# The causal mask of the row maxima: from TensorE's accumulation to VectorE's maximum pass, with another order of steps

## The chip, the cores and the metric

The kernel runs on one core of a Trainium2 chip. The time is device time in microseconds (us) from one launch to its end; the lower the better. Every time below was measured on the chip, and every row comes from one profiled execution.

## What is computed

Cross attention with a causal mask and a residual, then a feed-forward layer with a residual, for x and a context of shape (16, 512, 512) in fp32, 16 heads of width 32. Cut to what matters here:

```python
scores = einsum('bhsd,bhtd->bhst', qh, kh) * scale
mask = triu(ones((Sq, Sq), dtype=bool), k=0).at[0, 0].set(False)   # the diagonal is masked too, but for (0, 0)
scores = where(mask, -inf, scores)
probs = softmax(scores, axis=-1)
out = einsum('bhst,bhtd->bhsd', probs, vh)
x = x + (out @ Wo.T + bo)          # q from layernorm(x), k and v from the context
x = x + ffn(layernorm(x))          # ternary weights, relu squared; not touched by the change
```

## The kernel before

The kernel has two phases, one after the other: attention for all 16 batches (`attention_phase`), then the feed-forward layer for all 16 (`ffn_phase`). Only the first is touched.

**Two passes over the scores.** The 16 heads are worked in 4 groups of 4. For each group the scores are computed twice. The first pass (steps `S`, function `s_unit`) has queries on the partitions and is used only for the maximum of every row. The maxima of a group, 16 columns of `maxima`, are then transposed by TensorE (step `M`, L637), split into a high and a low part by ScalarE (L707) and VectorE (L768), and sent by two DMAs (step `SEND`, L711) into rows 96 and 97 of the stacked operands. The second pass (steps `T`, `t_unit`, L534) has keys on the partitions, subtracts the maximum by those two rows, and goes through ScalarE's exponential (L742) and a mask on GpSimd (L435) into `probs`; steps `PV` multiply by V.

**A score unit.** Only blocks on or below the diagonal are computed. They are packed into units of 512 columns, one PSUM bank each, 10 units a group (`UNITS`), 40 a batch. In a half group (two heads) units 0 and 2 hold the 512 columns of a head's last query block, units 1 and 3 hold 384 and 128 columns (its third and its first block), and unit 4 holds 256 columns of each head (the second block). The same pattern of columns repeats for units 5 to 9. The two banks `s_bank` alternate: TensorE may start unit u once VectorE has signalled `s_free` for unit u-2.

**Where the mask is.** After the score products of a unit, TensorE accumulates `ident_bf` times `masks` (bf16, entries 0 or -1e30) onto the blocks at the diagonal (L513): 128 columns in units 0 and 2, 256 in the others. VectorE then takes maxima from PSUM with `tensor_reduce`: one of 512 (L804), or 384 and 128 (L807, L808), or one over two runs of 256 (L811).

**The order.** Each engine runs the same list of steps, `batch_steps` (written out by hand, L59 to L88), and picks out its own work; each engine is in order, and semaphores tie them together. VectorE's list passes through `low_parts_later`, which moves the low part (L778) of a Q, K, XT or CT step behind the next `S` step where such a step comes soon. `PART` is a third of a Q, K or V product (4 of its 12 matmuls), so that score units can stand between the thirds. `STACK` (SyncE) copies Q and K from `stage` into the stacked operands with six DMAs for two heads (L353); `S` units 0 and 5 of a group wait for them. `ONES`, `NT`, `NR`, `NB`, `NM`, `NH`, `NL` are the normalisation by the row sums (`NT` L831, `NR` L834, `NB` L838), `LN_*` and `XT`/`CT` prepare the next batch, `OA`/`OC`/`OB` are the output projection. So ("S", 3, 4) is unit 4 of group 3.

Of the kernel before, what the change touches and what calls it, by code (L numbers as in the profile page):

```python
# [12 lines left out]
P = 128  # L13
# [4 lines left out]
MASKED = -1e30  # L18
UNITS = 10
# [36 lines left out]
def batch_steps(more):  # L56

    steps = [
# [3 lines left out]
        ("STACK", 1, 0), ("M", 0), ("V", 2), ("SEND", 0), ("PART", "Q", 2, 0), ("STACK", 1, 1), ("PART", "Q", 2, 1),  # L62
# [26 lines left out]
    ]  # L89
    return steps if more else [s for s in steps if not is_next(s, True) and s[0] not in ("X_LOAD", "C_LOAD")]  # L90
# [103 lines left out]
def attention_phase(nc, dram, batches):  # L194
# [14 lines left out]
    with ExitStack() as c:  # L209
# [25 lines left out]
        ident_bf = sb("ident_bf", [P, P], BF16)  # L235
        masks = sb("masks", [P, 3, P], BF16)
# [51 lines left out]
        CONSTS = 12  # L288
# [119 lines left out]
        def _(pool):  # L408
# [3 lines left out]
            consts.inc(pool.memset(ident_bf[:, :], 0.0))  # L412
            consts.inc(pool.memset(masks[:, :, :], 0.0))
# [3 lines left out]
            for m in (ident, ident_bf):  # L417
                consts.inc(pool.affine_select(out=m[:, :], in_=m[:, :], compare_op=ALU.not_equal, fill=1.0,
                                              base=0, pattern=[[-1, P]], channel_multiplier=1))

            consts.inc(pool.affine_select(out=masks[:, 2, :], in_=masks[:, 2, :], compare_op=ALU.is_ge, fill=MASKED,
                                          base=0, pattern=[[-(P + 1), P]], channel_multiplier=P))
            for m in range(2):
                consts.inc(pool.affine_select(out=masks[:, m, :], in_=masks[:, m, :], compare_op=ALU.is_ge,
                                              fill=MASKED, base=-1, pattern=[[-1, P]], channel_multiplier=1))
# [67 lines left out]
        def _(pe):  # L493
# [9 lines left out]
            def s_unit(g, k, out):  # L503
                st = stack[g % 2]
                pair, u = divmod(k, 5)

                def block(h, r, t1, cols, start=True):

                    pe.matmul(out[:, cols:cols + t1], st[0:96, QS, h, P * r:P * r + P], st[0:96, KS, h, 0:t1],  # L509
                              start=start, stop=False, skip_group_check=True)  # L510

                def mask(view, added):
                    return pe.matmul(view, ident_bf[:, :], added, start=False, stop=True, skip_group_check=True)  # L513

                if u < 4 and u % 2 == 0:
                    block(2 * pair + u // 2, 3, 512, 0)
                    return mask(out[:, 384:512], masks[:, 0, :])
                if u < 4:  # L520
                    block(2 * pair + u // 2, 2, 384, 0)
                    block(2 * pair + u // 2, 0, 128, 384, start=False)
                    return mask(out[:, 256:512], masks[:, 1:3, :].rearrange("p m x -> p (m x)"))
                block(2 * pair, 1, 256, 0)
                block(2 * pair + 1, 1, 256, 256, start=False)
                return mask(out[:, :].rearrange("p (h t) -> p h t", h=2)[:, :, P:2 * P], masks[:, 0:2, :])
# [889 lines left out]
```

## Time and profile before

| | |
|---|---|
| median of 3 runs | 2728.15 us (2727.88 to 2735.14) |
| the profiled execution, its own time | 2733.87 us |
| its span, first to last instruction | 2732.2 us |
| mean granted TensorE clock | 0.978 of full |
| TensorE matmuls, busy | 2611.6 us (96%) |
| VectorE busy | 1596.1 us (58%) |
| ScalarE busy | 1031.2 us (38%) |
| GpSimd busy | 840.9 us (31%) |

The attention phase fills roughly the first 1570 us of the span. Busy time of a matmul counts from its start to its modelled end, and neighbouring matmuls overlap; so what a matmul adds to the time is read from the distance between the ends of neighbours in a timeline, not from its duration. The same holds, to a smaller degree, for VectorE. In a timeline the first number is the start and the second the time taken; a row with "xN" merges N instructions.

### The profile page before, as it was taken

The numbers are of one execution on the slowest core, as the hardware profiler recorded it, in microseconds if no ns is written. First come the engines' busy times: TensorE is split into PE (matmuls) and PEld (weight loads), VectorE is DVE, ScalarE is ACT, GpSimd is POOL, SyncE is SP. The second block draws the span as 40 slices with busy tenths as digits, with TensorE's granted clock in tenths as the row PEclk, the third lists the DMA queues.
The fourth block names the chain that finished last, engine by engine and source line by source line (L and its number), as shares of the span: only waits on it lengthen the run. The fifth ranks groups of instructions, "written<-read, shape, count | busy, mean of one in ns | idle before, by whom it ended". The sixth has DMA issues, their size and how long they took to land. (4 is left out here: it accounts for less than half of the span.)

```text
span 2732.2 us, 45231 instructions
## 1 busy us (share of the span) xinstructions
PE 2611.6 (96%) x14258; PEld 1943.7 (71%) x14258; DVE 1596.1 (58%) x3166; ACT 1031.2 (38%) x1903; POOL 840.9 (31%) x1559
## 2 busy tenths in 40 slices
PE   7999999999999999999999949999999999999998
PEld 5676667667766766776676537888888888888887
DVE  4675676667667666766765474444444444444454
ACT  2433433343343334334433454333333333333332
POOL 1643654474356346445644600000000000000000
PEclk9999999999999999999999868999999999999999
DMA  4344254344435433533444240000000000000000
GB/s 149 84 123 124 68 148 116 91 102 130 117 75 141 116 104 89 141 113 82 128 116 112 52 156 16 31 31 31 31 31 31 31 31 31 31 31 31 31 31 31
DMA packets 125252, 215.58 MB, mean 79 GB/s; under 512 B 20244, under 2 KB 22292, under 8 KB 124709
## 3 DMA queue, kind: packets, MB, share of 16 engines
q1 hardware_dynamic: 121124, 214.14, 28.0%
q10 hardware_dynamic: 4096, 1.06, 0.2%
q8 instruction: 16, 0.26, 0.0%
q14 instruction: 16, 0.12, 0.0%
HBM read 79.86 MB, written 33.55 MB: 42 GB/s over the span
## 5 line engine op out<-in xcount | busy, mean ns | idle before, releaser
L742 ACT ACTIVATE probs<-bank 128x512 f32<-128x512 f32 x640 | 359.2, 596 | 316.0 <-PE bank L534 310.7
L1159 PE MATMUL y_bank<-projT,a_hi 128*128 128x512 f32 x1024 | 409.1, 399 | 0.0
L1147 PE MATMUL h_bank<-x2T_hi,fcT 128*128 128x512 f32 x1024 | 406.4, 397 | 0.9 <-ACT scale_row L1230 0.9
L1148 PE MATMUL h_bank<-x2T_lo,fcT 128*128 128x512 f32 x1024 | 406.9, 397 | 0.0
L1161 PE MATMUL y_bank<-projT,a_lo 128*128 128x512 f32 x1024 | 403.9, 394 | 0.0
L1074 POOL COPY x_res<-x_in_sb 128x512 f32<-128x512 f32 x64 | 53.7, 879 | 1030.4 <-DVE y_sb L1376 967.9
L1238 ACT ACTIVATE relu<-h_bank,scale_fc 128x512 f32<-128x512 f32 x256 | 175.9, 687 | 503.5 <-PE h_bank L1151 503.5
L1349 DVE CAST a_hi<-act_sq 128x512 fp32r<-128x512 f32 x256 | 120.8, 472 | 372.5 <-ACT act_sq L1243 372.5
L435 POOL TENSOR_SCALAR_AFFINE_SELECT probs<-probs 128x256 f32<-128x256 f32 (+1 forms) x640 | 228.1, 367 | 250.8 <-ACT probs L742 244.4
L509 PE MATMUL bank<-stack 96*128 96x512 f32 (+3 forms) x1024 | 268.9, 340 | 19.5 <-DMA stack<-stage 15.5
L534 PE MATMUL bank<-stack 98*128 98x512 f32 (+3 forms) x1024 | 267.4, 346 | 17.0 <-DMA stack<-m_stage 15.9
L804 DVE TENSOR_REDUCE maxima<-bank 128x1 f32<-128x512 f32 x256 | 175.9, 687 | 142.6 <-PE bank L513 139.2
L534 PEld LDWEIGHTS bank<-stack 98*128 98x128 f32 x1024 | 175.6, 196 | 91.5 <-ACT probs L742 47.0
L477 POOL TENSOR_TENSOR x_res<-x_res,bias_sb 128x512 f32<-128x512 f32 x64 | 80.4, 1288 | 519.1 <-DMA x_res<-in_x_dram 455.1
L509 PEld LDWEIGHTS bank<-stack 96*128 96x128 f32 x1024 | 180.1, 195 | 74.4 <-issue 31.2
L1148 PEld LDWEIGHTS h_bank<-x2T_lo,fcT 128*128 128x128 f32 x1024 | 193.3, 189 | 47.2
L1147 PEld LDWEIGHTS h_bank<-x2T_hi,fcT 128*128 128x128 f32 x1024 | 193.1, 189 | 47.3 <-issue 1.1
L1161 PEld LDWEIGHTS y_bank<-projT,a_lo 128*128 128x128 f32 x1024 | 192.4, 188 | 43.3
L1159 PEld LDWEIGHTS y_bank<-projT,a_hi 128*128 128x128 f32 x1024 | 192.4, 188 | 43.2
L727 ACT ACTIVATE stage<-bank 128x512 fp32r<-128x512 f32 x128 | 76.5, 598 | 314.5 <-PE bank L500 289.8
L453 POOL TENSOR_TENSOR acc<-probs 128x384 f32<-128x384 f32 x192 | 189.8, 1009 | 11.7 <-POOL probs L435 7.4
L1351 DVE TENSOR_TENSOR a_lo<-act_sq,a_hi 128x512 fp32r<-128x512 f32 x256 | 185.9, 726 | 8.8
(187 smaller groups left out, 4922.1 us busy)
## 6 DMA issues: line engine op xcount, KB each, us to landing
stack<-stage SPq DMA_DIRECT2D x768, 128.0 KB, 2.3
xc_rows<-in_x_dram SPq DMA_DIRECT2D x16, 1024.0 KB, 5.3
x_res<-in_x_dram SPq DMA_DIRECT2D x16, 1024.0 KB, 5.5
x<-x_res SPq DMA_DIRECT2D x64, 256.0 KB, 2.2
x_in_sb<-x SPq DMA_DIRECT2D x16, 1024.0 KB, 5.6
out_dram<-y_sb SPq DMA_DIRECT2D x64, 256.0 KB, 2.0
xc_rows<-in_ctx_dram SPq DMA_DIRECT2D x15, 1024.0 KB, 5.3
stack<-m_stage ACTq DMA_DIRECT2D x128, 8.0 KB, 2.2
```

What stands on the lines that cost most here:

```text
L435: return pool.affine_select(out=view, in_=view, compare_op=ALU.is_ge, fill=0.0, base=0 if first_block else -1, pattern=([[0, count]] if co ...
L453: chain.inc(pool.tensor_tensor(acc[:, h, P:S], probs[:, u0, P:S], probs[:, u1, 0:S - P], ALU.add))
L509: pe.matmul(out[:, cols:cols + t1], st[0:96, QS, h, P * r:P * r + P], st[0:96, KS, h, 0:t1], start=start, stop=False, skip_group_check=True)
L534: return pe.matmul(out[:, cols:cols + S - P * r], st[0:98, KS, h, P * r:P * r + P], st[0:98, QS, h, P * r:S], start=True, stop=True)
L742: act.activation(probs[:, s[2], :], t_bank[u % 2][:, :], ACT.Exp, scale=SCALE).then_inc(exp_done, 1)
L804: last = dve.tensor_reduce(maxima[:, col + 3:col + 4], bank_u[:, :], AX.X, ALU.max)
L1147: pe.matmul(h_bank[b % 2][:, :], fcT[:, k, cols], xT_hi[:, k, :], start=k == 0, stop=False)
L1148: pe.matmul(h_bank[b % 2][:, :], fcT[:, k, cols], xT_lo[:, k, :], start=False, stop=False)
L1159: pe.matmul(y_bank[j][:, :], a_hi[:, b % RING, P * j:P * j + P], projT[:, b, :], start=b == 0, stop=False)
L1161: last = pe.matmul(y_bank[j][:, :], a_lo[:, b % RING, P * j:P * j + P], projT[:, b, :], start=False, stop=b == NB - 1)
L1238: act.activation(relu[:, b % 2, :], h_bank[b % 2][:, :], ACT.Relu, scale=scale_fc[:, b:b + 1]).then_inc(relu_done, 1)
L1351: dve.tensor_tensor(a_lo[:, b % RING, :], act_sq[:, b % 2, :], a_hi[:, b % RING, :].bitcast(F32), ALU.subtract).then_inc(hid_ready, 1)
```

## The change

The 640 mask matmuls (40 a batch) are gone. `s_unit` now issues only score products, and each is a finished product of its own. VectorE adds the mask itself: each `tensor_reduce` becomes a `tensor_tensor_reduce` that adds a bf16 mask tile from SBUF (`causal`, of which the last 128 columns hold the triangle and the rest zeros, or `causal_first` for the first block), writes the sum back to the same PSUM columns, and leaves its maximum over the row in `maxima`. Unit 4 and unit 9, which one instruction covered before, take two. Each of these instructions is followed on VectorE by a second one that puts the accumulated maximum into its column. VectorE waits for `s_full` with a wait of its own ahead of the instruction (`wait_alone`).

The list of steps is written anew as well. Only pieces of it are shown.

```diff
-        ("STACK", 1, 0), ("M", 0), ("V", 2), ("SEND", 0), ("PART", "Q", 2, 0), ("STACK", 1, 1), ("PART", "Q", 2, 1),
-        ("T", 0, 0), ("T", 0, 1), ("X_LOAD",), ("S", 1, 0), ("S", 1, 1), ("Q", 2), ("T", 0, 2), ("S", 1, 2),
...
+        ("STACK", 1, 0), ("M", 0), ("V", 2), ("SEND", 0), ("PART", "Q", 2, 0), ("STACK", 1, 1), ("T", 0, 0),
+        ("PART", "Q", 2, 1), ("T", 0, 1), ("S", 1, 0), ("T", 0, 2), ("S", 1, 1), ("Q", 2), ("S", 1, 2), ("S", 1, 3),
...
-        ident_bf = sb("ident_bf", [P, P], BF16)
-        masks = sb("masks", [P, 3, P], BF16)
+        causal = sb("causal", [P, S], BF16)
+        causal_first = sb("causal_first", [P, P], BF16)
...
-                    block(2 * pair + u // 2, 3, 512, 0)
-                    return mask(out[:, 384:512], masks[:, 0, :])
+                    return block(2 * pair + u // 2, 3, 0)
...
-                    block(2 * pair + u // 2, 2, 384, 0)
-                    block(2 * pair + u // 2, 0, 128, 384, start=False)
-                    return mask(out[:, 256:512], masks[:, 1:3, :].rearrange("p m x -> p (m x)"))
-                block(2 * pair, 1, 256, 0)
-                block(2 * pair + 1, 1, 256, 256, start=False)
-                return mask(out[:, :].rearrange("p (h t) -> p h t", h=2)[:, :, P:2 * P], masks[:, 0:2, :])
+                    block(2 * pair + u // 2, 2, 0)
+                    return block(2 * pair + u // 2, 0, 384)
+                block(2 * pair, 1, 0)
+                return block(2 * pair + 1, 1, 256)
...
-                        dve.wait_ge(s_full, i * SB + u + 1)
+                        wait_alone(dve, dve_passed, (s_full, i * SB + u + 1))
+
+                        def row_max(h, r, cols):
+
+                            t1 = P * r + P
+                            added = causal_first[:, :] if r == 0 else causal[:, S - t1:S]
+                            return dve.tensor_tensor_reduce(
+                                out=bank_u[:, cols:cols + t1], in0=bank_u[:, cols:cols + t1], in1=added, scale=1.0,
+                                scalar=LOWEST, op0=ALU.add, op1=ALU.max,
+                                accum_out=maxima[:, 4 * h + r:4 * h + r + 1])
+
                         if k < 4 and k % 2 == 0:
-                            col = 4 * (2 * pair + k // 2)
-                            last = dve.tensor_reduce(maxima[:, col + 3:col + 4], bank_u[:, :], AX.X, ALU.max)
+                            last = row_max(2 * pair + k // 2, 3, 0)
                         elif k < 4:
-                            col = 4 * (2 * pair + k // 2)
-                            dve.tensor_reduce(maxima[:, col + 2:col + 3], bank_u[:, 0:384], AX.X, ALU.max)
-                            last = dve.tensor_reduce(maxima[:, col:col + 1], bank_u[:, 384:512], AX.X, ALU.max)
+                            row_max(2 * pair + k // 2, 2, 0)
+                            last = row_max(2 * pair + k // 2, 0, 384)
                         else:
-                            col = 8 * pair + 1
-                            last = dve.tensor_reduce(maxima[:, col:col + 5:4],
-                                                     bank_u[:, :].rearrange("p (h t) -> p h t", h=2), AX.X, ALU.max)
+                            row_max(2 * pair, 1, 0)
+                            last = row_max(2 * pair + 1, 1, 256)
                         last.then_inc(s_free, 1)
```

**Place A: TensorE, group 3, from unit 4 on.** L509 is a score product (banks 2 and 3 are the two score banks), L513 the mask, L534 (L526 after) a product of the second pass of group 2, L499 after and L500 before a product of Q for the next batch. Before:

```order
L509 MATMUL bank2<-stack1 128x256 x2
L513 MATMUL bank2<-masks,ident_bf 128x2x128
L534 MATMUL bank5<-stack0 128x512
L632 REGISTER_ALU
L509 MATMUL bank3<-stack1 128x512
L513 MATMUL bank3<-masks,ident_bf 128x128
L534 MATMUL bank4<-stack0 128x384
L534 MATMUL bank4<-stack0 128x128
L632 REGISTER_ALU
L509 MATMUL bank2<-stack1 128x384
L509 MATMUL bank2<-stack1 128x128
L513 MATMUL bank2<-masks,ident_bf 128x256
```

After, the same units 4, 5 and 6:

```order
L499 MATMUL bank1<-xT_hi,wT_hi 128x512
L499 MATMUL bank1<-xT_lo,wT_hi 128x512
L624 REGISTER_ALU
L509 MATMUL bank2<-stack1 128x256 x2
L526 MATMUL bank4<-stack0 128x384
L526 MATMUL bank4<-stack0 128x128
L624 REGISTER_ALU
L509 MATMUL bank3<-stack1 128x512
L624 REGISTER_ALU
L509 MATMUL bank2<-stack1 128x384
L509 MATMUL bank2<-stack1 128x128
L526 MATMUL bank5<-stack0 128x512
```

The second third of Q stood between units 7 and 8 before; now it stands ahead of unit 4, and from unit 4 to unit 9 at most one unit of the second pass stands between two score units.

**Place B: VectorE, group 2, up to the low part of the maxima (`m_stage`).** `stage` is the low part of K for group 3, `xT_lo` of x for the next batch, `o_recip` and `o_small` are `NT` and `NR` of group 0. Before:

```order
L807 TENSOR_REDUCE maxima<-bank2 128x1
L808 TENSOR_REDUCE maxima<-bank2 128x1
L801 REGISTER_ALU
L811 TENSOR_REDUCE maxima<-bank3 128x2
L777 REGISTER_ALU
L778 TENSOR_TENSOR stage<-bank0,stage 128x512
L777 REGISTER_ALU
L778 TENSOR_TENSOR xT_lo<-bank1,xT_hi 128x512
L767 REGISTER_ALU
L768 TENSOR_TENSOR m_stage<-bank2,m_stage 16x128
```

After, where the low part of K has just gone ahead of these rows:

```order
L799 ISA bank3,maxima<-bank3,causal 128x256
L799 ISA maxima 128x1
L799 ISA bank3,maxima<-bank3,causal 128x256
L799 ISA maxima 128x1
L769 REGISTER_ALU
L770 TENSOR_TENSOR xT_lo<-bank1,xT_hi 128x512
L827 ISA
L830 STREAM_TRANSPOSE o_recip<-bank7 128x512
L833 RECIPROCAL o_small<-o_recip 128x16
L759 REGISTER_ALU
L760 TENSOR_TENSOR m_stage<-bank2,m_stage 16x128
```

The low part of K moved from behind unit 9 to ahead of it, and `NT` and `NR` of group 0 moved from behind the low part of the maxima to ahead of it. Each of the two new instructions of unit 9 has a second one behind it.

## Rows read from the trace of the kernel before

**Rows 1.** Busy time by stretch: one batch, and group 3's units 0 to 9.

```profile
core 0: us, PE busy (x) PEld busy (x) DVE busy (x) ACT busy (x) POOL busy (x), PEclk, DMA share, GB/s
683.22:692.73 9.51, 9.23 (x57) 6.44 (x56) 7.86 (x16) 5.59 (x10) 6.89 (x14) 1.00 0.58 169
646.00:740.80 94.80, 91.94 (x582) 64.33 (x581) 63.30 (x127) 36.83 (x72) 48.20 (x92) 1.00 0.42 111
```

**Rows 2.** Groups by line, whole span: busy, mean ns | idle before.

```profile
L804 DVE TENSOR_REDUCE maxima<-bank 128x1 f32<-128x512 f32 x256 | 175.9, 687 | 142.6 <-PE bank L513 139.2
L513 PE MATMUL bank<-masks,ident_bf 128*128 128x256 bf16 (+1 forms) x640 | 170.6, 267 | 0.0
```

**Rows 3.** Timeline of TensorE, group 2: score units with their masks.

```profile
671.78 0.40 PE L534 MATMUL bank<-stack 98*128 98x384 f32 x2
672.02 0.45 PE L509 MATMUL bank<-stack 96*128 96x512 f32 x1
672.31 0.23 PE L513 MATMUL bank<-masks,ident_bf 128*128 128x128 bf16 x1
672.35 0.47 PE L500 MATMUL bank<-cT_lo,wT_hi 128*128 128x512 f32 x1
672.66 0.39 PE L500 MATMUL bank<-cT_hi,wT_lo 128*128 128x512 f32 x1
...
673.36 0.40 PE L509 MATMUL bank<-stack 96*128 96x384 f32 x2
673.60 0.28 PE L513 MATMUL bank<-masks,ident_bf 128*128 128x256 bf16 x1
673.64 0.48 PE L500 MATMUL bank<-cT_hi,wT_lo 128*128 128x512 f32 x1
```

**Rows 4.** Timeline of VectorE, group 0: four instructions with no idle between.

```profile
639.36 0.68 DVE L778 TENSOR_TENSOR stage<-bank,stage 128x512 fp32r<-128x512 f32 x1
639.96 0.55 DVE L807 TENSOR_REDUCE maxima<-bank 128x1 f32<-128x384 f32 x1
640.43 0.28 DVE L808 TENSOR_REDUCE maxima<-bank 128x1 f32<-128x128 f32 x1
640.62 0.69 DVE L811 TENSOR_REDUCE maxima<-bank 128x2 f32<-128x512 f32 x1
```

**Rows 5.** Timelines: small instructions of VectorE, an accumulator read of ScalarE.

```profile
9.04 0.38 DVE L166 BATCH_NORM_AGGREGATE ln_mean_var<-ln_stats 128x2 f32<-128x6 f32 x4
...
1594.73 0.61 ACT L1183 ACTIVATE relu<-w_nat 128x512 f32<-128x512 f32 x1
1595.25 0.18 ACT L1183 ACTIVATION_READ_ACCUMULATOR relu<-w_nat 128x1 f32 x1
```

**Rows 6.** Group of a VectorE instruction with two tensor sources and a scalar.

```profile
L1291 DVE SCALAR_TENSOR_TENSOR tern<-w_nat,half,neg 128x512 bf16<-128x512 f32 x12 | 8.5, 748 | 0.7 <-PE h_bank L1093 0.5
```

**Rows 7.** Timeline of TensorE: maxima transposed, then the second pass (groups 0, 3).

```profile
642.12 0.27 PE L637 MATMUL bank<-ident,maxima 128*128 128x128 f32 x1
...
646.81 0.64 PE L534 MATMUL bank<-stack 98*128 98x512 f32 x3
...
693.82 0.33 PE L637 MATMUL bank<-ident,maxima 128*128 128x128 f32 x1 [0.15 <-DVE maxima L811]
...
697.92 0.73 PE L534 MATMUL bank<-stack 98*128 98x512 f32 x3 [0.58 <-DMA stack<-m_stage]
```

**Rows 8.** Timelines of TensorE, VectorE and SyncE's queue: group 2 to 3.

```profile
674.42 0.39 PE L500 MATMUL bank<-cT_hi,wT_lo 128*128 128x512 f32 x1
676.74 1.06 PE L554 MATMUL bank<-probs,v_sb 128*32 128x512 f32 x8 [0.46 <-POOL probs L435]
680.86 0.50 PE L534 MATMUL bank<-stack 98*128 98x512 f32 x1 [0.31 <-DMA stack<-m_stage]
682.66 0.49 PE L509 MATMUL bank<-stack 96*128 96x512 f32 x1 [0.86 <-DMA stack<-stage]
...
675.81 0.68 DVE L778 TENSOR_TENSOR stage<-bank,stage 128x512 fp32r<-128x512 f32 x1
677.17 0.27 DVE L768 TENSOR_TENSOR m_stage<-bank,m_stage 16x128 fp32r<-16x128 f32 x1
...
676.76 7.25 SPq L353 DMA_DIRECT2D stack<-stage  x11
```

More of the change, by code:

```diff
@@ L18 @@
 MASKED = -1e30
+LOWEST = -3.0e38
 UNITS = 10
@@ L58, in batch_steps @@
     steps = [
[1 row of a table removed]
[1 row of a table added]
         ("Q", 1), ("S", 0, 3), ("S", 0, 4), ("PART", "K", 1, 0), ("S", 0, 5), ("PART", "K", 1, 1), ("S", 0, 6),
         ("K", 1), ("S", 0, 7), ("S", 0, 8), ("PART", "V", 1, 0), ("S", 0, 9), ("PART", "V", 1, 1), ("V", 1),
-        ("STACK", 1, 0), ("M", 0), ("V", 2), ("SEND", 0), ("PART", "Q", 2, 0), ("STACK", 1, 1), ("PART", "Q", 2, 1),
[26 rows of a table removed]
[4 rows of a table added]
+        ("T", 0, 8), ("PART", "V", 3, 0), ("STACK", 2, 0), ("T", 0, 9), ("LN_STATS", 1), ("LN_STATS", 2),
[22 rows of a table added]
     ]
@@ L286, in attention_phase @@
         act_passed = sem("act_passed")
-        CONSTS = 12
+        CONSTS = 10
         HI_SKIP = sum(s[0] == "V" for s in STEADY)
@@ L411, in _ @@
             consts.inc(pool.memset(ident[:, :], 0.0))
-            consts.inc(pool.memset(ident_bf[:, :], 0.0))
-            consts.inc(pool.memset(masks[:, :, :], 0.0))
+            consts.inc(pool.memset(causal[:, :], 0.0))
+            consts.inc(pool.memset(causal_first[:, :], 0.0))
             consts.inc(pool.memset(ones[:, :], 1.0))
@@ L416, in _ @@
             pool.wait_ge(consts_ready, consts.now())
[L417 to L425, printed above, removed]
+            consts.inc(pool.affine_select(out=ident[:, :], in_=ident[:, :], compare_op=ALU.not_equal, fill=1.0,
+                                          base=0, pattern=[[-1, P]], channel_multiplier=1))
+            consts.inc(pool.affine_select(out=causal_first[:, :], in_=causal_first[:, :], compare_op=ALU.is_ge,
+                                          fill=MASKED, base=0, pattern=[[-(P + 1), P]], channel_multiplier=P))
+            consts.inc(pool.affine_select(out=causal[:, S - P:S], in_=causal[:, S - P:S], compare_op=ALU.is_ge,
+                                          fill=MASKED, base=-1, pattern=[[-1, P]], channel_multiplier=1))
             for s in range(2):
@@ L505, in s_unit, with block @@
                 pair, u = divmod(k, 5)
[L507 to L513, printed above, removed]
+                def block(h, r, cols):
+                    t1 = P * r + P
+                    return pe.matmul(out[:, cols:cols + t1], st[0:96, QS, h, P * r:P * r + P], st[0:96, KS, h, 0:t1],
+                                     start=True, stop=True)
                 if u < 4 and u % 2 == 0:
-                    block(2 * pair + u // 2, 3, 512, 0)
-                    return mask(out[:, 384:512], masks[:, 0, :])
+                    return block(2 * pair + u // 2, 3, 0)
                 if u < 4:
-                    block(2 * pair + u // 2, 2, 384, 0)
-                    block(2 * pair + u // 2, 0, 128, 384, start=False)
-                    return mask(out[:, 256:512], masks[:, 1:3, :].rearrange("p m x -> p (m x)"))
-                block(2 * pair, 1, 256, 0)
-                block(2 * pair + 1, 1, 256, 256, start=False)
-                return mask(out[:, :].rearrange("p (h t) -> p h t", h=2)[:, :, P:2 * P], masks[:, 0:2, :])
+                    block(2 * pair + u // 2, 2, 0)
+                    return block(2 * pair + u // 2, 0, 384)
+                block(2 * pair, 1, 0)
+                return block(2 * pair + 1, 1, 256)
             def t_unit(g, k, out):
@@ L800, in program @@
                         pair, k = divmod(s[2], 5)
-                        dve.wait_ge(s_full, i * SB + u + 1)
+                        wait_alone(dve, dve_passed, (s_full, i * SB + u + 1))
+                        def row_max(h, r, cols):
+                            t1 = P * r + P
+                            added = causal_first[:, :] if r == 0 else causal[:, S - t1:S]
[3 more added lines that the diff above has]
+                                accum_out=maxima[:, 4 * h + r:4 * h + r + 1])
                         if k < 4 and k % 2 == 0:
-                            col = 4 * (2 * pair + k // 2)
-                            last = dve.tensor_reduce(maxima[:, col + 3:col + 4], bank_u[:, :], AX.X, ALU.max)
+                            last = row_max(2 * pair + k // 2, 3, 0)
                         elif k < 4:
-                            col = 4 * (2 * pair + k // 2)
-                            dve.tensor_reduce(maxima[:, col + 2:col + 3], bank_u[:, 0:384], AX.X, ALU.max)
-                            last = dve.tensor_reduce(maxima[:, col:col + 1], bank_u[:, 384:512], AX.X, ALU.max)
-                        else:
-                            col = 8 * pair + 1
-                            last = dve.tensor_reduce(maxima[:, col:col + 5:4],
-                                                     bank_u[:, :].rearrange("p (h t) -> p h t", h=2), AX.X, ALU.max)
+                            row_max(2 * pair + k // 2, 2, 0)
+                            last = row_max(2 * pair + k // 2, 0, 384)
+                        else:
+                            row_max(2 * pair, 1, 0)
+                            last = row_max(2 * pair + 1, 1, 256)
                         last.then_inc(s_free, 1)
```

51 rows, old and new, of the table steps are left out of this document.

## Prediction

> **What bounds the kernel now.** I read the page first (which engine is busy, and where), then the busy time by stretch, then the groups by line, and last the timelines around the score units. The stretch of one batch [rows 1] is 94.8 us long; TensorE is busy in 91.94 of it at the full clock (granted 1.00, its 2.4 GHz level), VectorE in 63.3, ScalarE in 36.8. So in the attention phase TensorE is the bound, idle for 2.9 us a batch, and VectorE has a third of its time free. That free time is not even: while group 3's ten score units run, VectorE is busy 7.86 us out of 9.51 [rows 1], 83%. What comes off TensorE comes off the time, unless VectorE is late where the units stand close. The feed-forward phase is untouched.
>
> **What the mask matmuls cost.** Their busy time is 170.6 us [rows 2], but they overlap their neighbours. I take the distances between ends (start plus time taken) [rows 3]. Two plain 512-column matmuls end at 672.82 and 673.05: 0.23 us apart. The 512-column score product ends at 672.47, its 128-column mask at 672.54 (+0.07), the next 512-column matmul at 672.82 (+0.28 where 0.23 is usual). So a 128-column mask costs 0.07 + 0.05 = 0.12 us; 16 a batch (units 0, 2, 5, 7 of 4 groups) make 1.9 us. A 256-column mask ends at 673.88, after products that end at 673.76, and its successor ends at 674.12: 0.12 us and no delay behind it. The 8 in units 4 and 9 save 0.12 each, 1.0 us. In units 1, 3, 6 and 8, 16 a batch, the mask follows a 128-column product. Without it the next long matmul follows that short one directly, and from 384 + 128 columns (end 672.18) to the end of the next 512 (672.47) it is 0.29, not 0.23. So 0.06 comes back, and each saves 0.06: 1.0 us. Sum: 3.9 us. The rows are rounded to 0.01, which over 40 units allows 0.4 either way; I take 4.0 us a batch, or 64 us over 16 batches.
>
> **What VectorE pays.** Back to back, ends lie 0.47 us apart for 384 elements, 0.20 for 128 and 0.60 for 512 [rows 4], and one L804 takes 687 ns alone [rows 2]. Elements cost 1.05 ns each by these (0.27 us for 256 more), so 256 take 0.33. An addition of two tensors from PSUM and SBUF (L778, first of [rows 4]) takes 0.68, no more than a reduction. The new main instruction with its write to PSUM and its bf16 mask is not in the trace. From below it costs the same 0.60. From above: an instruction with two tensor sources and a scalar takes 748 ns, 61 more than L804 [rows 6], and the worst is half the rate, 1.05 ns more per element. I take the same as before. Units 4 and 9 now take two instructions: 8 x 0.06 = 0.5 us a batch. Then there is the read of the accumulator behind each of the 64 instructions a batch. ScalarE's read of this kind moves the end from 1595.34 to 1595.43, 0.09 us, though it takes 0.18 in itself [rows 5]. Four small instructions of VectorE take 0.38 together, about 0.08 each [rows 5]. I take 0.09, with bounds of 0.06 (hidden but for its issue) and 0.20 (its whole duration, not overlapped). That is 64 x 0.09 = 5.8 us a batch. VectorE then has 63.3 + 6.3 = 69.6 us of work in some 92: on average hidden, and the cover goes only where units stand close. In the place of 0.60, 0.66 and 0.60 a unit now takes 0.69, 0.84 and 0.84 us (units 0/2, 1/3, 4).
>
> The Trainium skill (Vector Engine (DVE) Microarchitecture Reference, section Points that are easy to get wrong) says that an instruction of the two-source accumulating form halves its throughput when both sources are in SBUF and not bf16. Here one source is in PSUM and the other is bf16, so by its words the full rate stays; the row of 748 ns, with one fp32 and one bf16 source in SBUF, agrees with a full rate there. The Trainium skill (VectorE: DVE Perf Modes, section Two Vector instructions with no wait between them) says that an accumulator output is two instructions, and that the second is held until the first has finished only where their start quadrants change. All tiles here start at partition 0, so by the rule the read overlaps and is nearer the 0.09 than the 0.20; no row of VectorE shows it.
>
> **Where the order makes TensorE wait, per batch.**
>
> (a) Group 0, from `M` to the second pass. Before, 4.69 us pass from L637 to L534 with no wait. In group 3, where the second pass waits for `m_stage`'s DMA, it is 4.10 us [rows 7]. The new order moves a third of Q (4 x 0.23 = 0.92) behind the first unit: 3.77 us of work against 4.10. Cost 0.3 us.
>
> (b) Group 2 to group 3 (place B). Count from the end of K's last matmul, 674.81 [rows 8]. Before, the low part of K ended at 676.49 (+1.68), SyncE issued its six DMAs from 676.76 on (0.66 each), and group 3's first score unit started at 682.66 (+7.85), with idle times of 0.46, 0.31 and 0.86 on the way: 1.63 together. After, a unit of the second pass and score unit 8 come first (0.58), VectorE takes unit 8 (0.84) and then the low part (0.60) with some 0.07 of signalling: +2.09, so 0.41 later, and the DMAs put the score unit at +8.26. On the other path, unit 9 (0.84) ends at +2.93, the low part of x at +3.53, `NT` (0.60) and `NR` (0.29), which now stand ahead, at +4.42, the low part of the maxima at +4.61. From there it took 680.86 - 677.44 = 3.42 us to the second pass: +8.03, and the score unit at +8.27. Both say 8.3. TensorE's own work in between is 7.85 - 1.63 = 6.22, plus 0.58, minus the last transpose of x (0.6) and a mask (0.13): 6.07. Idle 2.2 instead of 1.6. Cost 0.6 us. The waits of `PV` for GpSimd lie inside this and cost nothing of their own.
>
> (c) Group 3, units 4 to 9 (place A). Let unit 4 be full at 0. VectorE frees it at 0.84, does `NR` (0.29), frees unit 5 at 1.82, unit 6 at 2.66, unit 7 at 3.35, unit 8 at 4.19, unit 9 at 5.03. TensorE could start unit 6 at 0.51 and must wait until 0.9; unit 7 at 1.42, waits until 1.9; unit 8 at 2.43, waits until 2.75; unit 9 at 3.3, waits until 3.45; it ends at 3.7, the last third of Q (0.92) at 4.6, and `M` waits until 5.1 for unit 9. Without waits `M` would come at 2.06 + 0.24 + 0.92 = 3.2. So 1.9 us of waiting, in place of the 0.28 of idle in that stretch [rows 1] and 0.15 before `M` [rows 7]. Cost 1.5 us.
>
> In groups 0 to 2 the same count gives 1.15 us or more of TensorE work between the units that share a bank, against 0.69 to 0.84 (1.44 with a low part between), and the double buffer covers the rest. X_LOAD and C_LOAD are moved in the list but stand between the same steps of SyncE as before. They cost nothing.
>
> **Sum.** 4.0 - 0.3 - 0.6 - 1.5 = 1.6 us a batch, 26 us over 16. The profiled execution took 2733.87 us, its span 2732.2, so it would be near 2708. It lies 5.7 us above the median of the runs, 2728.15. On that scale the forecast is 2702 us. A difference below 0.3% (8 us) can't be told from none by such a measurement.
>
> **Rivals.**
>
> R1, the waits don't come: the waits of (a) to (c) are shorter than counted, as the new read costs 0.06 and VectorE's signals reach TensorE sooner. Then up to 4.0 us a batch is kept: 2728 - 64 = 2664, and with half of the waits 2683. For it: the counts in (c) are sums of many small numbers. Against it: (a) and (b) hang on DMAs and not on the read.
>
> R2, the accumulator read is not overlapped, 0.20 us (slower). The extra 0.11 is paid 10 times in (c) (1.1 us), 4 times in (b) (0.4), and groups 0 and 1 now run out of cover: counted over the list, VectorE has 11.4 and 12.5 us between units 0 and 9, TensorE 8.8 and 9.1 and about 1.5 from the double buffer, so 1.1 and 1.9 more. Together 4.5 us, so 1.6 - 4.5 = -2.9 a batch: 2728 + 46 = 2774. It decides from about 0.13 us a read on, where the gain is gone. For it: ScalarE's read takes 0.18 in itself. Against it: only 0.09 of that shows between ends.
>
> R3, the main instruction runs at half rate. 20,480 elements a batch at 1.05 ns more are 21.5 us: VectorE has 91 us, and at each group's units it has 15 to 16 us against 10.3 to 12.2. That adds 19 us of waiting: 15 us a batch worse, 2728 + 240 = 2968. Nothing in [rows 6] speaks for it.
>
> R4, it does what it says and gains nothing: the saved 4.0 us of TensorE is given back in full by waits like (c) in every group, near 2728. For it: TensorE's idle time of 2.9 us a batch hangs on DMA chains that do not shrink. Against it: those chains are two of the four groups' hand-overs, and are counted.
>
> **How the numbers follow.** Forecast 0.55 (2690 to 2715), R1 0.16, R2 0.14, R3 0.05, R4 0.10. Faster by over 0.3%: the forecast, R1, little else: 0.71. Within 0.3%: R4 and an edge of the forecast: 0.11. Slower: R2, R3: 0.18. The range leaves out R3, the far ends of R1 and R2: 2668 to 2768. Its own range for the likeliest case is 2688 to 2716.
>
> **What would show it.** Right: the profile after has 640 matmuls less; a batch of about 93.2 us; VectorE near 69 us of it; ends of a main instruction and its read 0.69 us apart for 512 elements; idle of about 1.9 us from unit 4 of group 3 to `M`, 2.2 us up to group 3's first unit, 0.3 us ahead of group 0's second pass. Wrong: reads that move the ends by over 0.13 us; idle on TensorE ahead of score units in groups 0 and 1; a step for 512 elements above 0.8 us.

## The result: 0.4% slower, where 1% faster was forecast

| | median, us | runs | against before (95% interval) |
|---|---|---|---|
| before | 2728.9 | 19 (2721.27 to 2735.14) | |
| after | 2738.6 | 19 (2730.74 to 2746.4) | 1.0038 (1.003 to 1.0046) |
| forecast | 2702 (2668 to 2768) | | |

The time lies inside the range and on the other side of before. The span of the profiled execution is 2735.1 us. Its page, engines and slices:

```profile
PE 2568.8 (94%) x13618; PEld 1915.2 (70%) x13618; DVE 1622.1 (59%) x4318; ACT 1031.1 (38%) x1903; POOL 842.7 (31%) x1557
...
PEclk9999999999999999999999968999999999999999
```

640 matmuls are gone, TensorE's busy time fell by 43 us, the granted clock is the same, and the span grew by 3. So TensorE waits more. The busy time by stretch, one batch after the change and group 3's score units (columns as in [rows 1]):

```profile
646.00:741.65 95.65, 89.54 (x541) 62.77 (x540) 64.49 (x199) 36.82 (x72) 48.82 (x93) 1.00 0.42 111
682.15:691.83 9.68, 8.96 (x52) 6.57 (x50) 8.55 (x29) 5.99 (x12) 7.45 (x15) 1.00 0.53 165
```

Against [rows 1], TensorE is busy 2.4 us less a batch and idle 6.1 instead of 2.9; VectorE's busy time grew by only 1.2 us a batch, and it still has 31 us free. The groups by line say what VectorE now does:

```profile
L799 DVE CUSTOM_DVE_ANT_0 bank<-bank,causal 128x512 f32<-128x512 f32 x256 | 180.0, 703 | 144.5 <-PE bank L509 141.4 <-DVE ln_rstd L184 1.4
L799 DVE DVE_READ_ACCUMULATOR2_ANT maxima<- 128x1 f32 x1024 | 144.8, 141 | 0.0
L799 DVE CUSTOM_DVE_ANT_0 bank<-bank,causal 128x256 f32<-128x256 f32 x256 | 105.4, 453 | 16.7 <-PE bank L509 16.1 <-issue 0.2
```

The full rate holds: 703 ns for 512 elements against 687 in [rows 2]. Who made TensorE's weight loads wait between 100 and 1550 us (columns: us in total, times, longest), before:

```profile
PEld bank L534 <- DMA stack<-m_stage: 30.4, 32, 2.2
...
PEld bank L509 <- DVE maxima L804: 15.4, 26, 0.8
```

and after:

```profile
PEld bank L509 <- DVE maxima L799: 70.4, 147, 0.9
PEld bank L526 <- DMA stack<-m_stage: 52.1, 48, 2.3
...
PEld bank L629 <- DVE maxima L799: 42.4, 43, 2.1
```

Score products now wait for VectorE to free a bank, 147 times instead of 26 for L804 (and some more for L808): 10 times a batch, half a microsecond each. The waits for the maxima's DMA and of the transposition of the maxima (L629) grew too. Idle on TensorE ahead of score units in groups 0 and 1 is one of the signs by which the prediction said that it would be wrong.

**Work and waits.** Idle time understates waits, since a matmul's modelled duration (0.45) is longer than its step (0.23). So I split each batch in another way. For every pair of neighbouring matmuls I took the distance between their ends, and called work the smallest distance (5th percentile) that the traces have for this pair of kinds; the rest is wait. Means over 11 batches of the profiled executions, in us a batch; "score waits" are those ahead of score products, by the group they belong to (group 3's include the wait for `STACK`'s DMAs):

| | period | work | wait | score waits, groups 0, 1, 2, 3 | ahead of `T` in group 0 |
|---|---|---|---|---|---|
| before | 95.0 | 88.6 | 6.4 | 0, 0, 0.26, 1.68 | 0 |
| after | 95.7 | 84.0 | 11.7 | 1.53, 0.97, 0.41, 2.01 | 0.87 |
| forecast, difference | -1.6 | -4.0 | +2.4 | none in groups 0 to 2 | +0.3 |
| measured, difference | +0.7 | -4.6 | +5.2 | +1.5, +1.0, +0.2, +0.3 | +0.9 |

The work went as forecast and a little more. The waits grew twice as much as forecast. The experiments ask why: is it VectorE's turn (theory A) or the new list of steps (theory B)? A third cause, that VectorE's longer program has to be loaded again in every batch, was not among the theories; it is read from the same traces behind the experiments.

### The profile page after: what moved, and what is told of

It reads as the page before. It is cut to its first block and busy times, and to the rows that moved or that the text cites. A ratio compares the mean times of both kernels' runs of the same rounds, so it can differ in the third digit from the quotient of the medians.

```text
span 2735.1 us, 45739 instructions
## 1 busy us (share of the span) xinstructions
PE 2568.8 (94%) x13618; PEld 1915.2 (70%) x13618; DVE 1622.1 (59%) x4318; ACT 1031.1 (38%) x1903; POOL 842.7 (31%) x1557
## 3 DMA queue, kind: packets, MB, share of 16 engines
q10 hardware_dynamic: 4096, 1.06, 0.2%
## 5 line engine op out<-in xcount | busy, mean ns | idle before, releaser
L799 DVE CUSTOM_DVE_ANT_0 bank<-bank,causal 128x512 f32<-128x512 f32 (+2 forms) x768 | 424.2, 575 | 198.6 <-PE bank L509 186.1
L509 PE MATMUL bank<-stack 96*128 96x512 f32 (+3 forms) x1024 | 269.5, 341 | 30.6 <-DVE maxima L799 11.3
L526 PE MATMUL bank<-stack 98*128 98x512 f32 (+3 forms) x1024 | 255.9, 334 | 32.5 <-DMA stack<-m_stage 32.2
L509 PEld LDWEIGHTS bank<-stack 96*128 96x128 f32 x1024 | 174.0, 190 | 124.1 <-DVE maxima L799 74.8
L526 PEld LDWEIGHTS bank<-stack 98*128 98x128 f32 x1024 | 173.2, 190 | 117.9 <-DMA stack<-m_stage 53.0
L452 POOL TENSOR_TENSOR acc<-probs 128x384 f32<-128x384 f32 x192 | 189.8, 1010 | 11.7 <-POOL probs L434 7.4
```

Source lines behind the costliest of these rows:

```text
L452: chain.inc(pool.tensor_tensor(acc[:, h, P:S], probs[:, u0, P:S], probs[:, u1, 0:S - P], ALU.add))
L509: return pe.matmul(out[:, cols:cols + t1], st[0:96, QS, h, P * r:P * r + P], st[0:96, KS, h, 0:t1], start=True, stop=True)
L526: return pe.matmul(out[:, cols:cols + S - P * r], st[0:98, KS, h, P * r:P * r + P], st[0:98, QS, h, P * r:S], start=True, stop=True)
L799: return dve.tensor_tensor_reduce(out=bank_u[:, cols:cols + t1], in0=bank_u[:, cols:cols + t1], in1=added, scale=1.0, scalar=LOWEST, op0=A ...
```

## The experiments

Each time stands beside runs of before on the same chip (medians 2728.1 to 2728.6); the ratio's interval is in parentheses.

**e2: the changed body, the old list.**

```diff
 def batch_steps(more):
     steps = [
-        (the new list)
+        (the list of before)
```

> The changed kernel with the old list of steps; the rest of the change stays. Theory A (what a score unit's bank costs in turn-round time grew: VectorE now starts 0.2 us after TensorE's product instead of 0.04, because the wait is an instruction of its own, and the accumulator reads add 0.06 each): the old list has score units closer together, so this is no faster than the changed kernel, 2740 to 2760 us. Theory B (the new list itself costs: less work between the transposed maxima and the second pass, NT and NR ahead of the maxima's low part): with the old list this is 1 us a batch or more faster than the changed kernel, 2715 to 2725 us.

Measured: 2727.8 us, 0.9998 (0.9987 to 1.0008). With its old list the body of the change costs nothing and gains nothing; the new list costs 11 us on top. The time lies between the two theories' numbers: B has the sign right. But the saved work is still missing.

**e3: the old body, the new list.**

```diff
-        (the list of before)
+        (the new list)
```

> The kernel before (masks by TensorE, plain reductions) with the new list of steps alone. Theory A: VectorE's turn is as short as ever and the new spacing only helps it, so within 8 us of before, 2721 to 2737. Theory B: the new list costs 0.3 us in group 0's hand-over, 0.5 in group 2's and some in group 3, 1.2 us a batch: 2740 to 2755.

Measured: 2728.6 us, 1.0001 (0.9991 to 1.0012), theory A's number. Work and wait are 88.2 and 7.0. The new list's hand-overs do cost here (0.47 us ahead of group 0's `T`, 1.23 at the maxima of group 2 against 0.33), but some of it comes back elsewhere. On the old body, with the masks on TensorE, the list costs nothing.

**e4: the old body with the new form of wait.**

```diff
-                        dve.wait_ge(s_full, i * SB + u + 1)
+                        wait_alone(dve, dve_passed, (s_full, i * SB + u + 1))
```

> The kernel before with only the form of VectorE's wait for a score unit changed: a wait of its own ahead of the first reduction, with a semaphore increment, as in the changed kernel. Theory A: VectorE starts about 0.17 us later after each unit that it waits for; TensorE waits 0.5 to 1.2 us more a batch, 2737 to 2748. Rival (the form of the wait costs nothing, the later start in the changed kernel comes from the new instruction itself): within 4 us of before.

Measured: 2735.0 us, 1.0026 (1.0012 to 1.004), a little under theory A's range. A wait that is an instruction of its own costs 6 us without anything else. The timelines show how. Before the change, TensorE's mask ends at 647.80 and VectorE's reduction starts at 647.84:

```profile
647.57 0.23 PE L513 MATMUL bank<-masks,ident_bf 128*128 128x128 bf16 x1
```

```profile
647.84 0.69 DVE L804 TENSOR_REDUCE maxima<-bank 128x1 f32<-128x512 f32 x1 [1.96 <-PE bank L513]
```

In e4 the mask ends at 646.21 and the same reduction starts at 646.36, 0.15 instead of 0.04 later:

```profile
645.98 0.23 PE L513 MATMUL bank<-masks,ident_bf 128*128 128x128 bf16 x1
```

```profile
646.36 0.69 DVE L804 TENSOR_REDUCE maxima<-bank 128x1 f32<-128x512 f32 x1 [2.07 <-PE bank L513]
```

**e5: no mask in the first pass.** What is subtracted then covers the masked scores of the diagonal blocks too; softmax does not depend on it as long as no exponential leaves the range of fp32, and the second pass masks as ever.

```diff
                 if u < 4 and u % 2 == 0:
-                    block(2 * pair + u // 2, 3, 512, 0)
-                    return mask(out[:, 384:512], masks[:, 0, :])
+                    return block(2 * pair + u // 2, 3, 512, 0)
```

(and so for the other units)

> The kernel before without any mask in the first pass: no mask matmuls, plain reductions, old list. A row's subtracted maximum then covers the masked scores of its diagonal block too; softmax does not depend on what is subtracted, and the second pass masks as before. It measures the mask matmuls alone. If TensorE's work is the bound where they stand: 4.2 us a batch less, some given back as waits, 2665 to 2680. If chains that do not pass through TensorE's work set the time (the saving turns into waits whatever VectorE does): 2710 to 2729.

Measured: 2684.2 us, 0.9841 (0.9821 to 0.9861), just above the range. Work 84.3 a batch, 4.2 less than before, as the ends in [rows 3] give it; waits 8.0, 1.6 more. TensorE's work is the bound, and nearly two thirds of what is taken from it shows. So the reason given for R4, DMA chains that do not shrink, is refuted. Its outcome is not: in the change itself the saved work does come back in full as waits (4.6 and 5.2 us a batch, and e2 at 2727.8 us).

**e7: e5 with the wait of its own.** The edit of e4 on e5.

> The kernel before without any mask in the first pass (what is subtracted then covers masked scores of the diagonal block, which softmax does not depend on), with VectorE's wait for a score unit as an instruction of its own. Without that form of wait it took 2684 us. Theory A: the form of the wait costs 6 to 12 us here as it cost 6 with the masks, 2690 to 2697; the rest of the way to 2728 (the changed kernel's body in the old order) is then the new instruction with its reads. Rival: with TensorE less loaded the late starts matter much more, the form of the wait carries most of the 44 us, 2710 to 2725.

Measured: 2694.7 us, 0.9879 (0.9856 to 0.9901): 10.5 us over e5, theory A's number. The two intervals just touch (four runs each), so the size of this step is rough.

**e9: e7 with the pieces of the change and a small instruction behind each.** Its masks are left out as in e5.

```diff
+                            dve.tensor_reduce(maxima[:, 4 * h + r:4 * h + r + 1], bank_u[:, cols:cols + t1], AX.X,
+                                              ALU.max)
+                            place = 16 * s[1] + 4 * h + r
+                            return dve.tensor_scalar(small[:, place:place + 1], ones[:, 0:1], 1.0, None, ALU.mult)
```

> No mask in the first pass (softmax does not depend on what is subtracted), old list, separate wait, and plain reductions in the pieces of the change (64 a batch), each followed by a one-column multiplication of VectorE in the place of the accumulator read. Without the small instructions and the split it took 2695 us, with the real add-and-maximum 2728. Theory A (the reads and the split pay the 33 us, as instructions on a path that turns every bank): 2712 to 2728. Rival (the add-and-maximum itself is the dear part, by its later start or its write to PSUM): 2695 to 2705.

Measured: 2734.9 us, 1.0023 (1.0012 to 1.0035), 40 us over e7 and above theory A's range. Plain reductions with 64 small instructions a batch and units 4 and 9 split cost as much as the real thing (e2: 2727.8). The add-and-maximum itself is not dear; what follows it is, and yet it moves the ends only by 0.06:

```profile
646.59 0.69 DVE L800 TENSOR_REDUCE maxima<-bank 128x1 f32<-128x512 f32 x1 [1.99 <-PE bank L510]
647.20 0.14 DVE L803 TENSOR_SCALAR small<-ones 128x1 f32<-128x1 f32 x1
647.26 0.55 DVE L800 TENSOR_REDUCE maxima<-bank 128x1 f32<-128x384 f32 x1
647.73 0.14 DVE L803 TENSOR_SCALAR small<-ones 128x1 f32<-128x1 f32 x1
```

Ends: 647.28, 647.34, 647.81, 647.87. The 64 small ones are 3.8 us of VectorE's time a batch, and the period is 2.6 us longer than in e7. They delay `s_free`, which every score product waits for, and everything behind it in VectorE's queue. But 1.5 of the 2.6 us are waits ahead of the first five score units of group 0, which e7 does not have, and they have another cause (see "What the longer program of VectorE brings with it"). e9 changes the small instructions and the split together; which of the two carries how much was not tried.

**e1b: the changed kernel, the wait carried by a small instruction.**

```diff
-                        wait_alone(dve, dve_passed, (s_full, i * SB + u + 1))
+                        dve.wait_ge(s_full, i * SB + u + 1)
+                        dve.tensor_scalar(ticket[:, u:u + 1], ones[:, 0:1], 1.0, None, ALU.mult)
```

> The changed kernel, but the wait for a score unit is carried by a one-column multiplication of VectorE ahead of the first add-and-maximum, and not by an instruction of its own. Theory A: the reaction falls from 0.2 us to about 0.10 (0.04 and one small instruction of 0.06), each waiting unit's bank is free 0.1 us earlier, 2729 to 2735 us. Rival (the new instruction starts late whatever holds it, and the small one is only more work): 2739 to 2748.

Measured: 2734.4 us, 1.0018 (1.0003 to 1.0033), inside theory A's range and 4 us under the changed kernel, whose interval it overlaps: a gain is likely and not shown. The change's own instruction with the wait on it was not tried.

**e8: the changed kernel with two places of its list put back.**

```diff
-        ("PART", "Q", 2, 0), ("STACK", 1, 1), ("T", 0, 0), ("PART", "Q", 2, 1), ("T", 0, 1),
+        ("PART", "Q", 2, 0), ("STACK", 1, 1), ("PART", "Q", 2, 1), ("T", 0, 0), ("T", 0, 1),
...
-        ("XT", 0), ("NT", 0), ("STACK", 3, 0), ("NR", 0), ("T", 1, 9), ("M", 2), ("NB", 0),
+        ("XT", 0), ("STACK", 3, 0), ("T", 1, 9), ("M", 2), ("NT", 0), ("NR", 0), ("NB", 0),
```

> The changed kernel with two places of its list put back: the second third of Q for group 2 stands ahead of the second pass's first unit again, and NT and NR of group 0 stand behind the transposed maxima of group 2 again; the spacing of the score units stays. Theory B (these two hand-overs carry the 11 us by which the old list is faster with this body): 2727 to 2731. Rival (the spacing in groups 0 and 3 carries it): 2735 to 2740.

Measured: 2730.8 us, 1.0013 (1.0002 to 1.0025), theory B's number. Of the 11 us that the new list costs, about 8 were in these two hand-overs.

**e11: the changed kernel again.** No edit.

> The changed kernel once more, beside the others on one chip: 2735 to 2741 us, 7 to 12 above before, by both theories; it fixes the distance to the kernel with two places put back (2731), which Theory B wants at 5 us or more.

Measured: 2743.8 us, 1.0058 (1.004 to 1.0076), above the expected 2735 to 2741. This is 5 us over the first measurement of the same kernel, so a difference of less than that between two kernels measured at different times should not be leaned on. The distance to e8 holds, on the side that theory B wants.

**e6 and e10: no mask, with the new list, and with e8's list.** The lists of after and of e8 on the body of e5.

> The kernel before without any mask in the first pass and with the new list of steps. If the new list costs by its hand-overs (theory B): 0.5 to 0.9 us a batch over the same body in the old list (2684), 2692 to 2699. If the list costs only together with VectorE's longer turn (theory A): 2680 to 2688.

> No mask in the first pass, plain reductions, and the new list with its two hand-overs put back as before (second third of Q ahead of the second pass of group 0; NT and NR behind the maxima of group 2). The old list took 2684 us with this body and the new one 2700. If the hand-overs carry that difference: 2682 to 2690. If the spacing of the score units does: 2694 to 2700.

Measured: e6 2699.9 us, 0.9899 (0.9876 to 0.9921), 1 us over theory B's range; e10 2684.9 us, 0.9842 (0.9818 to 0.9865), as expected if the hand-overs carry it. With a short turn on VectorE the new list costs 16 us, all of it in the two hand-overs. The wider spacing of the score units is worth nothing here (e10 against e5), which refutes theory A's reading of e6.

**e12: no mask, the old list with two moves.**

```diff
-        ("T", 0, 0), ("T", 0, 1), ("X_LOAD",), ("S", 1, 0), ("S", 1, 1), ("Q", 2),
+        ("S", 1, 0), ("T", 0, 0), ("T", 0, 1), ("X_LOAD",), ("S", 1, 1), ("Q", 2),
...
-        ("S", 3, 3), ("S", 3, 4), ("NR", 1), ("T", 2, 5), ("S", 3, 5),
+        ("S", 3, 3), ("T", 2, 5), ("S", 3, 4), ("NR", 1), ("S", 3, 5),
```

> No mask in the first pass, plain reductions, old list with two moves: group 1's first score unit ahead of the second pass's first unit, where TensorE waited 0.7 us a batch for the maxima's DMA, and unit 5 of the second pass between score units 3 and 4 of group 3. If TensorE's waits there are filled: 0.3 to 0.8 us a batch under 2684, 2672 to 2680. If the waits only move on to the next hand-over: 2682 to 2688.

Measured: 2682.4 us, 0.9829 (0.9808 to 0.9851), not told apart from e5. Its waits are 7.95 a batch against 8.0: they moved on. It and e5 beat both kernels.

**What the longer program of VectorE brings with it.** The attention phase runs 15 of its 16 batches as a loop, whose body each engine executes again. The profile lists the DMA packets that carry instructions. Before:

```profile
q14 instruction: 16, 0.12, 0.0%
```

and after:

```profile
q14 instruction: 86, 0.70, 0.1%
```

The 70 more are 5 packets of 8 KB for each of the 14 jumps back to the head of the loop; before, there is no such packet inside the loop. All six kernels with the accumulator reads or the small instructions (after, e2, e8, e9, e11, e1b) have 86, all eight others 15 or 16. VectorE's list is what decides: e9 differs from e7 on VectorE alone, and the profile records 334 instructions of VectorE a batch in the six, at most 262 in the others (e4, e7). Two stops of VectorE come with the packets. From its branch at the end of the loop to its next instruction 0.24 to 0.33 us pass in the eight kernels, 2.9 to 3.3 us in the six, at each of the 14 jumps. Then it stops again ahead of unit 1 of group 0. Before:

```profile
631.33 0.68 DVE L796 COPY v_sb<-bank 128x512 f32<-128x512 f32 x1
632.06 0.56 DVE L807 TENSOR_REDUCE maxima<-bank 128x1 f32<-128x384 f32 x1
```

After, where the product of unit 1 ended at 630.63 and the copy at 630.97:

```profile
630.28 0.69 DVE L788 COPY v_sb<-bank 128x512 f32<-128x512 f32 x1
632.01 0.57 DVE L799 CUSTOM_DVE_ANT_0 bank<-bank,causal 128x384 f32<-128x384 f32 x1 [1.05 <-PE bank L509]
```

The row names TensorE's bank as what ended the idle time, but that product had been done since 630.63: VectorE had nothing to wait for. What TensorE pays, in us a batch (means over 11 batches, as above):

| | packets a batch | VectorE's stop ahead of unit 1 | waits ahead of group 0's units 0, 3, 4 |
|---|---|---|---|
| before, e5, e7 | 0 | 0.06 or less | 0, 0, 0 |
| after | 5 | 0.95 | 0.61, 0.34, 0.36 |
| e2 | 5 | 1.02 | 0.62, 0.37, 0.36 |
| e9 | 5 | 1.06 | 0.61, 0.46, 0.37 |

Units 3 and 4 wait because VectorE is late with units 1 and 2. Unit 0 waits for `STACK`: the sixth of its copies lands 3.1 us after its issue in the six kernels and 2.34 in the eight, and the first instruction packet of the batch starts while it is under way, some 1.8 us ahead of the unit. That the packet is what holds the copy up is argued from this timing alone. The rest is shown inside one kernel: in after's own first batch and its last, which no jump back precedes, VectorE starts unit 1 without a stop, and in the first batch no unit of these waits. No run kept the longer list and took the loading away.

The waits are 1.3 us a batch in after, 14 times: 18 us. As an estimate from them, and if all of it came back, the change would run near 2720 us without the loading, 0.3% faster than before.

**The way from before to after, in steps:** mask matmuls away -44.5 (e5), the wait of its own +10.5 (e7), the add-and-maximum with reads and split in place of plain reductions +33 (e2), of which some 20 are the waits of the last paragraphs (1.4 us, 14 times), the new list +11 (after). Sum: +10. The steps depend on their order: the new list costs nothing on the old body (e3) and 16 us without masks (e6).

## Why the prediction was wrong

**The work of the masks: right.** 4.0 us a batch forecast, 4.2 measured (e5), 4.6 with the new list.

**The prices on VectorE: right, a little high.** The main instruction costs as much between ends as a reduction, and the read 0.06 us, at the low bound of 0.06 to 0.20 (I took 0.09). R2 and R3 did not come. The Trainium skill's rule on the accumulator read (VectorE: DVE Perf Modes, section Two Vector instructions with no wait between them) agrees with the trace after: the read is an instruction of its own, and the 0.14 us that it takes overlap its neighbours. The Trainium skill's other rule, on halved throughput (Vector Engine (DVE) Microarchitecture Reference, section Points that are easy to get wrong), was rightly not applied: 703 ns.

**(b), the hand-over to group 3: right in its path.** K's last matmul ends at 673.26, and group 3's first score product starts 8.40 later (8.3 forecast). VectorE in the trace after:

```profile
674.71 0.69 DVE L770 TENSOR_TENSOR stage<-bank,stage 128x512 fp32r<-128x512 f32 x1
...
676.63 0.70 DVE L830 STREAM_TRANSPOSE o_recip<-bank 128x512 f32<-128x512 f32 x1
677.37 0.25 DVE L833 RECIPROCAL o_small<-o_recip 128x16 f32<-128x16 f32 x1
677.54 0.22 DVE L760 TENSOR_TENSOR m_stage<-bank,m_stage 16x128 fp32r<-16x128 f32 x1
```

The low part of K ends at +2.14 (2.09 forecast), the low part of the maxima at +4.50 (4.61).

**(c), group 3: right in its path.** From unit 4's product to the transposed maxima 5.1 us were forecast, and the trace has 5.1 (687.93 to 693.04). In part this is luck: the forecast left out VectorE's late reaction (0.19 us) and counted 0.29 us for `NR`, whose end comes 0.11 after the one ahead of it. The cost was put at 1.5 against the idle time of before; by work and wait it is about 1.1, as before had hidden waits there (0.5 ahead of unit 5, 0.4 ahead of `M`).

**(a): right in kind, too small.** 0.3 forecast, 0.9 measured. I took the 4.10 us of group 3 from maxima to second pass; in group 0 it took 4.4. The difference is the DMA: in the trace after, ScalarE issues it at 642.12 and the second pass starts at 645.38, 3.3 us later, while SyncE is issuing the stack copies; in group 3, with no copies about, it is 2.5 us (694.55 to 697.02).

```profile
642.12 1.22 ACTq L703 DMA_DIRECT2D stack<-m_stage  x2
...
694.55 1.16 ACTq L703 DMA_DIRECT2D stack<-m_stage  x2
...
639.23 7.68 SPq L355 DMA_DIRECT2D stack<-stage  x12
```

But the copies are about in group 0 before, too, and there the two DMAs landed 2.9 us after the issue and 4.09 after `M`, 0.6 ahead of the second pass (means over 11 batches; 2.4 after the issue in group 3). With the new list on the old body (e3) the second pass follows `M` by 4.09, as forecast. So the missing part comes with the new body, whose DMAs land 3.2 us after the issue, in e2 also. The loading is not needed for that, as it is 3.9 in e5; why it is later was not tested.

**The step that failed** is this one: "In groups 0 to 2 the same count gives 1.15 us or more of TensorE work between the units that share a bank, against 0.69 to 0.84 ..., and the double buffer covers the rest." It forecast no new waits in these groups, and they grew by 2.7 us a batch. Two things stand in its place.

The larger is a term that the prediction does not have: VectorE's program, longer by the reads, is loaded again in every batch of the loop. That makes 1.3 of the 1.5 us of group 0. I counted the reads by their time alone. R2 had expected waits in groups 0 and 1, but from reads of 0.20 us; they are 0.06.

The other, 1.1 us in groups 0 and 1, is a bank's turn. It is not VectorE's step. It goes from the end of one product to the end of the next in the same bank. The trace after, group 3's units 4 and 6, TensorE and then VectorE:

```profile
687.53 0.40 PE L509 MATMUL bank<-stack 96*128 96x256 f32 x2
...
689.05 0.50 PE L509 MATMUL bank<-stack 96*128 96x384 f32 x2 [0.60 <-DVE maxima L799]
```

```profile
688.12 0.43 DVE L799 CUSTOM_DVE_ANT_0 bank<-bank,causal 128x256 f32<-128x256 f32 x1 [0.60 <-PE bank L509]
688.47 0.14 DVE L799 DVE_READ_ACCUMULATOR2_ANT maxima<- 128x1 f32 x1
688.47 0.47 DVE L799 CUSTOM_DVE_ANT_0 bank<-bank,causal 128x256 f32<-128x256 f32 x1
688.85 0.14 DVE L799 DVE_READ_ACCUMULATOR2_ANT maxima<- 128x1 f32 x1
```

Product of unit 4 ends at 687.93; VectorE starts 0.19 later (the wait of its own), takes 0.87 to the end of the last read, 688.99; unit 6's product starts 0.06 later and takes 0.50: 1.62 us from end to end. Before the change the same turn, from unit 3 to unit 5 of group 3, is 0.04 + 0.75 + 0.06 + 0.57 (product and mask): 1.42. The new list leaves 1.15 us between such units, or 1.4 with the product's own step. That is 0.2 short at unit 8 of group 0 and unit 6 of group 1, which wait 0.17 and 0.19 us; at units 3 and 7 of group 1 VectorE is also still busy with the neighbour's bank, and they wait 0.34 and 0.37. The old list with its masks leaves 1.28 + 0.35, 0.2 to spare. I compared 1.15 with 0.84 and saw room. The missing terms are the reaction (0.19, which no row of before could show, as no wait there had this form, though I knew that it was added and gave it no price) and the product's own length in the chain (0.50, not its step of 0.23, which was in the rows).

**The second error** is of size: the waits came to 5.2 us instead of 2.4. Of the missing 2.8, 2.5 are the score waits of groups 0 and 1 (1.3 by the loading, 1.1 by the turns); the rest is (a), less what was overcounted in (c).

## What to carry to other kernels

A longer program can cost more than the time of its instructions. After a change that adds instructions to a loop, compare the instruction packets of the DMA queues in both profiles, and look at the first instructions behind the jump back; here 18 us lay there that no busy time shows.

Before moving work off the bound engine, count each shared buffer's turn from end to end: reaction, the consumer's instructions up to the last one that carries the signal, the way back, and the producer's full latency. Then compare that with the distance that the order leaves. An engine that is busy two thirds of the time can still be the one that is waited for. And look first for whether the work is needed at all: here the first pass could do without the mask, and leaving it out gave 1.6%.

## What the runs showed of the hardware

- With 334 recorded instructions of VectorE a batch, the loop over batches loads 5 instruction packets of 8 KB at each jump back, and VectorE goes on 2.9 to 3.3 us after its branch; with 222 or 262 there is no packet, and it goes on after 0.24 to 0.33 us. Some 5 us behind the branch it stops again, for 1.0 us.
- A wait that VectorE executes as an instruction of its own makes the next instruction start 0.15 to 0.19 us after the signal's matmul ends, where a wait carried by the instruction gives 0.04. Cost in this kernel: 6 us with the masks (e4), about 10 without (e7).
- The accumulator read of VectorE takes 0.14 us and moves the ends by 0.06, as any one-column instruction does (e9: also 0.14 and 0.06).
- VectorE adds a bf16 tile from SBUF to fp32 in PSUM, writes it back there and keeps the maximum at the rate of a plain reduction, 703 against 687 ns for 512 elements.
- A 128-column matmul is followed by a delay of 0.05 to 0.06 us before the next long one, with or without masks.
